# Layer 1 of a two-layer attention and expert network: splitting the expert weights beside the routing and straight into their slots, and a ring of three banks in its attention

## What is computed

```python
qkv = x @ w_qkv.T
o = _natten2d(q / D_HEAD ** 0.5, k, v, KSIZE)          # softmax over 7 x 7 keys
x = x + o @ w_out.T
...
shared_out = (silu(xf @ Wg_s) * (xf @ Wu_s)) @ Wd_s
logits = xf @ W_router + expert_bias
top_vals, top_idx = jax.lax.top_k(logits, 2)
rw = softmax(top_vals)
out_e = (silu(xf @ Wg_r[e]) * (xf @ Wu_r[e])) @ Wd_r[e]   # 384 -> 2 x 768 -> 384
routed_out = sum over the two chosen e of rw * out_e
```

## Time and profile before

| | us |
|---|---|
| median of three runs (1055.34 to 1055.71) | 1055.59 |
| the profiled execution | 1051.15 |
| its span, first to last instruction | 1049.4 |
| TensorE busy (93%) | 973.8 |
| VectorE / GpSimd / ScalarE busy | 544.5 / 519.5 / 322.8 |
| mean granted clock of TensorE | 0.978 |

### The profile page before, as it was taken

One profiled execution on the slowest core, in us unless ns is written; L12 is line 12 of the kernel. 1 busy time (PEld: TensorE's weight loads), 2 busy tenths in 40 slices (PEclk: granted clock), 3 DMA queues, 4 the chain that ended last, 5 costly groups with the idle time before them and its releaser, 6 DMA issues.

```text
span 1049.4 us, 14337 instructions
## 1 busy us (share of the span) xinstructions
PE 973.8 (93%) x4756; PEld 641.0 (61%) x4757; DVE 544.5 (52%) x960; ACT 322.8 (31%) x482; POOL 519.5 (50%) x375
## 2 busy tenths in 40 slices
PE   6999999999998999998598989699899999999998
PEld 3755555555546566665456555368666677677764
DVE  4466888888665355554555675871122222222224
ACT  2524455655721122221325555051111111111100
POOL 5614778898821122220634766646667667700014
PEclk9999999999998999999899999889999999999999
DMA  9679708000056357311435200504777777731015
GB/s 318 161 190 336 168 1 181 21 1 1 1 192 243 130 189 242 144 61 36 128 98 126 62 1 8 218 1 169 259 255 256 255 260 265 255 123 42 16 51 152
DMA packets 52493, 147.43 MB, mean 140 GB/s; under 512 B 7153, under 2 KB 26105, under 8 KB 52184
## 3 DMA queue, kind: packets, MB, share of 16 engines
q1 hardware_dynamic: 37080, 80.00, 25.1%
...
## 4 chain that ended last, share of the span: by engine, by line
PE 66%; POOL 13%; DVE 8%; DMA 7%; issue 4%; ACT 3%; DVEq 0%; SPq 0%; POOLq 0%; ACTq 0%
PE PS L2111 15%; PE PS L2133 8%; POOL raw L1026 6%; PE PS L1838 6%; PE PS L1874 6%; PE PS L1737 5%; PE PS L1894 5%; DMA raw<-in_Wg_r 5%; PE PS L1876 5%; PE PS L2016 3%; PE PS L2159 3%; POOL Wgu L1024 2%; DVE nmax L1426 2%; PE PS L1803 2%; PE PS L1748 2%
## 5 line engine op out<-in xcount | busy, mean ns | idle before, releaser
L1224 ACT ACTIVATE expS<-PS 128x1024 f32<-128x1024 f32 (+3 forms) x156 | 135.3, 877 | 106.4 <-PE PS L1876 104.8
L2133 PE MATMUL PS<-Wd,hidT 128*128 x414 | 142.8, 491 | 1.7 <-DVE hidT L1624 1.0
L953 POOL TENSOR_TENSOR exp_acc<-exp_acc,expS 128x512 f32<-128x512 f32 (+1 forms) x65 | 135.2, 2089 | 16.4 <-ACT expS L1224 14.7
L1874 PE MATMUL PS<-QA,KS 128*128 128x512 f32 (+3 forms) x312 | 116.5, 379 | 4.1 <-ACT QB L1202 3.5
L1426 DVE TENSOR_REDUCE nmax_part<-PS 128x1 f32<-128x512 f32 x160 | 105.5, 682 | 27.6 <-PE PS L1838 27.5
L1838 PE MATMUL PS<-KS,QA 128*128 128x512 f32 (+2 forms) x288 | 108.0, 401 | 9.5 <-DVE nmax L1426 5.1
L1876 PE MATMUL PS<-QB,KS 128*128 128x512 f32 (+3 forms) x312 | 109.9, 358 | 0.0
L2133 PEld LDWEIGHTS PS<-Wd,hidT 128*128 128x128 f32 x414 | 78.8, 192 | 48.9 <-issue 4.1
L2111 PE MATMUL PS<-Wgu,xbT_high 128*128 x207 | 91.1, 440 | 10.6 <-DMA Wgu_low<-raw 7.0
L2111 PE MATMUL PS<-Wgu,xbT 128*128 x276 | 97.4, 490 | 1.8 <-ACT xbT L1321 1.7
L1339 ACT ACTIVATE hidT<-PS 128x384 f32<-128x384 f32 x46 | 22.6, 491 | 236.3 <-PE PS L2119 236.3
...
...
...
## 6 DMA issues: line engine op xcount, KB each, us to landing
...
```

The costliest lines, as they stand in the source:

```text
L953: last = pool.tensor_tensor(acc, older, exp_tile(0, c, u)[:, pair, heads], ALU.add)
L1224: act.activation(exp_tile(layer, c, unit)[:, pair, :].rearrange("p (b n) -> p b n", b=2)[:, :, lo:hi], PS[:, 2 * pair:2 * pair + 2, lo:hi] ...
L1874: pe.matmul(PS[:, 2 * pair + j, lo:hi], keys, QA[layer][c % 2][:, g, queries], start=True, stop=False)
L2133: last = pe.matmul(PS[:, 7, 0:C], hidT[layer][:, par, i, :], Wd[layer][:, bass.ds(s, 1), i, :], start=i == 0, stop=i == m.IC - 1)
```

## The change

In the attention of layer 1 tiles, rows and sums now take turns in banks 4, 5 and 7 by a second list of the same kind. A block's first three tiles move one unit ahead, into unit 4 of the block before (`TILES_TO`; the first block that is made this way keeps `FIRST_TILES`); a unit has one tile behind each head's scores, and the rows stand behind the first pair of heads in unit 3. The reciprocal is cut in four, in units 2, 3 and 4 (two there). Both layers use one function `unit`.

For the expert weights, SyncE loads expert 0's gate weights during the last chunk of the attention (`raw_first_in`). GpSimd splits them once the first half of the tokens is normalised, and the up weights behind the shared expert's subtractions. From expert 1 on the subtraction writes straight into the low slot (`low_of`), no DMA places it, and a raw buffer is loaded again as soon as its part is subtracted; TensorE waits for `low_done`. The slots of high and low parts lie elsewhere for that, with the shared expert's high part now under expert 1's low slot.

```diff
@@ -475,16 +476,13 @@
         LEAD = 2
-        PIECES_TO = [0, 5, 10, 15, 16, 16]
+        FIRST_TILES = [0, 0, 5, 10, 15, 16]
+        TILES_TO = [0, 3, 7, 11, 15, 16]
         ROWS_AT = [6, 3]
         def keys_of(layer, qt):
             return (0, T) if layer == 0 else (max(qt - 1, 0) * P, min(qt + 2, NT) * P)
-
-        def pieces_at(hb, v):
-
-            return range(PIECES_TO[v], PIECES_TO[v + 1])
...
@@ -504,6 +502,11 @@
         def maxima_in(hb, v):
+            if hb >= BLOCKS:
+                ahead = hb + 1 if v < PER_HALF1 - 1 else hb + 2
+                cuts = FIRST_TILES if ahead == BLOCKS + 1 else TILES_TO
+                at = (v + 1) % PER_HALF1
+                return [(ahead, i) for i in range(cuts[at], cuts[at + 1])] if ahead < 2 * BLOCKS else []
...
@@ -513,15 +516,16 @@
             return [(ahead, i) for i in range(pieces(ahead) * at // per_half, pieces(ahead) * (at + 1) // per_half)]
-        ring = [("rows", 0, 0)]
-        for hb in range(BLOCKS):
-            for v in range(PER_HALF):
+        rings = [[("rows", 0, 0)], [("rows", BLOCKS, 0)]]
+        for hb in range(2 * BLOCKS):
+            la, n = hb // BLOCKS, hb % BLOCKS
+            for v in range((PER_HALF, PER_HALF1)[la]):
                 tiles = [("max",) + piece for piece in maxima_in(hb, v)]
-                rows = [("rows", hb + 1, 0)] if v == ROWS_AT[0] and hb + 1 < BLOCKS else []
-                totals = [("sums", hb - 1, 0)] if v == 1 and hb else []
-                ring += tiles[0:1] + tiles[1:2] + rows + tiles[2:4] + totals + tiles[4:]
+                rows = [("rows", hb + 1, 0)] if v == ROWS_AT[la] and n + 1 < BLOCKS else []
+                totals = [("sums", hb - 1, 0)] if v == 1 and n else []
+                rings[la] += tiles[0:2] + rows + tiles[2:4] + totals + tiles[4:]
         RING = [4, 5, 7]
-        ring_at = {item: n for n, item in enumerate(ring)}
+        ring_at = {item: n for ring in rings for n, item in enumerate(ring)}
...
@@ -566,8 +571,8 @@
             return (BLOCKS - 1 + TAIL_CUTS) * (hb // BLOCKS) + hb % BLOCKS
-        CUTS_AT = {3: [0], 4: [1], 5: [2], 6: [3]}
-        CUTS = [len(CUTS_AT), 1]
+        CUTS_AT = [{3: [0], 4: [1], 5: [2], 6: [3]}, {2: [0], 3: [1], 4: [2, 3]}]
+        CUTS = [4, 4]
...
@@ -831,6 +836,8 @@
             check(b_in[0], B_DMAS[1][2])
+            sp.wait_ge(score_psum, 2 * (PV_BEFORE[1] + 2 * U[1]))
+            sp.dma_start(raw_first[:, :, :].bitcast(F32), Wg_r[0].rearrange("(k p) n -> p k n", p=P)).then_inc(raw_first_in, 16)
...
@@ -1010,41 +1017,42 @@
                 def high_of(q, part):
-                    return Wgu[1][:, q % 2, 0, :, part * m.I:(part + 1) * m.I]
+                    return Wgu[1][:, q % 2, :, part * m.I:(part + 1) * m.I]
                 def load_raw(q, part):
                     pool.dma_start(raw_of(q, part)[:, :, :].bitcast(F32),
                                    (Wg_r, Wu_r)[part][q].rearrange("(k p) n -> p k n", p=P)).then_inc(raw_in[part], 16)
+                def low_of(q, part):
+
+                    low = Wgu_low[:, q % 2, 0:KC * 2 * m.I].rearrange("p (k n) -> p k n", k=KC)
+                    return low[:, :, part * m.I:(part + 1) * m.I]
+
                 def split(q, part):
                     own = raw_of(q, part)
-                    pool.wait_ge(raw_in[part], 16 * (q + 1))
+                    if (q, part) == (0, 0):
+                        pool.wait_ge(raw_first_in, 16)
+                    else:
+                        pool.wait_ge(raw_in[part], 16 * (q + part))
                     pool.tensor_copy(high_of(q, part), own[:, :, :].bitcast(F32)).then_inc(high_done, 1)
                     pool.wait_ge(high_done, 2 * q + part + 1)
-                    pool.tensor_tensor(own[:, :, :], own[:, :, :].bitcast(F32), high_of(q, part).bitcast(F32),
-                                       ALU.subtract).then_inc(low_done, 1)
-
-                def place_low(q, part):
-
-                    low = Wgu_low[:, q % 2, 0:KC * 2 * m.I].rearrange("p (k n) -> p k n", k=KC)
-                    pool.wait_ge(low_done, 2 * q + part + 1)
-                    pool.dma_start(low[:, :, part * m.I:(part + 1) * m.I].bitcast(F32), raw_of(q, part)[:, :, :].bitcast(F32)).then_inc(low_placed[part], 16)
-
-                def next_raw(q):
-
-                    for part in range(2):
-                        pool.wait_ge(low_placed[part], 16 * (q + 1))
-                        if q + 1 < E:
-                            load_raw(q + 1, part)
+                    pool.tensor_tensor(low_of(q, part) if q else own[:, :, :], own[:, :, :].bitcast(F32),
+                                       high_of(q, part).bitcast(F32), ALU.subtract).then_inc(low_done, 1)
+
+                def place_first_low(part):
+
+                    pool.wait_ge(low_done, part + 1)
+                    pool.dma_start(low_of(0, part).bitcast(F32), raw_of(0, part)[:, :, :].bitcast(F32)).then_inc(low_placed, 16)
                 def split_and_load(q):
                     for part in range(2):
                         split(q, part)
-                        place_low(q, part)
-                    next_raw(q)
+                        if q + 1 < E:
+                            pool.wait_ge(low_done, 2 * q + part + 1)
+                            load_raw(q + 1, part)
...
@@ -1053,14 +1061,14 @@
                     pool.wait_ge(normalised, normalised_before(2 * BLOCKS - 1) + TAIL_CUTS)
-                    for part in range(2):
-                        load_raw(0, part)
-                    for part in range(2):
-                        split(0, part)
+                    load_raw(0, 1)
+                    pool.wait_ge(xn_ready, 3 * NT + NT // HALF)
+                    split(0, 0)
                     for f in range(m.IC):
...
                                            ALU.subtract).then_inc(gu_lo_ready, 1)
+                    split(0, 1)
...
@@ -1079,8 +1087,10 @@
                     for part in range(2):
-                        place_low(0, part)
-                    next_raw(0)
+                        place_first_low(part)
+                    load_raw(1, 0)
+                    pool.wait_ge(low_placed, 16 * 2)
+                    load_raw(1, 1)
...
@@ -1475,22 +1485,17 @@
                     for v in range(U[layer] // HALF):
+                        for ahead, i in maxima_in(hb, v):
+                            maxima(ahead, [i])
+                            if layer == 0 and i == pieces(ahead) - 1:
+                                merge(ahead)
                         if layer == 0:
-                            for ahead, i in maxima_in(hb, v):
-                                maxima(ahead, [i])
-                                if i == pieces(ahead) - 1:
-                                    merge(ahead)
                             accumulate(hb, v)
-                            if hb > first_block:
-                                for cut in CUTS_AT.get(v, []):
-                                    reciprocals(hb - 1, CUTS[0], [cut])
-                            continue
-                        if hb + 1 < end_block:
-                            maxima(hb + 1, pieces_at(hb + 1, v))
-                            if v == ROWS_AT[1]:
-                                copy_rows(hb + 1)
-                        if v == ROWS_AT[1] and hb > first_block:
-                            reciprocals(hb - 1, 1, range(1))
+                        elif v == ROWS_AT[1] and hb + 1 < end_block:
+                            copy_rows(hb + 1)
+                        if hb > first_block:
+                            for cut in CUTS_AT[layer].get(v, []):
+                                reciprocals(hb - 1, CUTS[layer], [cut])
...
@@ -1846,10 +1848,8 @@
                         pe.wait_ge(max_done, max_before(hb + 1))
-                    bank = 4
-                    if layer == 0:
-                        bank_free(("rows", hb, 0))
-                        bank = ring_bank(("rows", hb, 0))
+                    bank_free(("rows", hb, 0))
+                    bank = ring_bank(("rows", hb, 0))
...
@@ -1963,48 +1966,17 @@
                             tile(2 * pair + j)
-                        if pair == 0 and v == ROWS_AT[0] and hb + 1 < BLOCKS:
+                        if pair == 0 and v == ROWS_AT[layer] and hb + 1 < first_block + BLOCKS:
                             maxima_rows(hb + 1)
                     weighted(c, u)
-                    if v == 1 and hb:
+                    if v == 1 and hb > first_block:
                         totals(hb - 1)
...
                     for u in range(U[layer]):
-                        if layer == 0:
-                            full_unit(c, u)
-                            continue
...
+                        unit(c, u)
...
@@ -2093,15 +2065,15 @@
                         if layer:
-                            for part in range(2):
-                                pe.wait_ge(low_placed[part], (q + 1) * 16)
```

(4 more changed lines are left out.)

75 lines of the change are left out of this document (25 added, 50 removed).

## The result

The changed kernel takes 1024.49 us (median of four runs, 1023.66 to 1025.49), the kernel before beside it 1055.65 (1055.34 to 1057.32): a ratio of 0.9702, 95% interval 0.9685 to 0.9719. Its profiled execution took 1025.49 us for a span of 1023.7.

What follows compares the result with a forecast made beforehand. The prediction took TensorE to bound the kernel nearly everywhere, so its gaps matter. Attention 5.0, expert 0's earlier start 4.6 and experts 10.0 sum to 19.6 us: 1055.59 becomes 1036.0, range 1029 to 1043.

Steps and rivals of the forecast that it cites:

- Part 1: Layer 1's attention: evenly placed VectorE work and earlier rows products remove 5.0 of 8.3 us of TensorE's recorded waits.
- TensorE's own is 17.25 less a fifth of 8.3, some 15.6: Attention block: TensorE's own work is its length less its recorded waits, above VectorE's 13.7 us, so TensorE stays the bound.
- bounds: 0 and 8.3 (no wait is left): Limits of the attention gain in us: VectorE as late at each tile as before, or every recorded wait gone.
- the walk: Stepping through a pair of attention blocks: TensorE 1.1 us ahead of VectorE in each of three blocks, 3.3 us of waits.
- Part 2: Normalisation: the second half's four VectorE instructions run unheld in 1.65 us; the first shared product starts 9.8 us sooner.
- Part 3: Routing: GpSimd's split holds VectorE's ranking, so of the earlier first shared product only 4.6 us reach expert 0.
- the hold misses the routing: Rival for the routing: VectorE gets through more often, expert 0 starts at 734.6, 4.8 us more gain, 1031.2; chance 0.14.
- The queue takes it back: Rival at expert 0: expert 1's load delays the second placement 5.4 us, 14.6 us gain remains, 1041.0; chance 0.10.
- Part 4: Routed experts: low parts go straight to their slots; six blocks take 65.2 us instead of 75.2, 10.0 gained.
- its last wait ends at 819.21: Routed experts before: TensorE waits no more after 819.21 us; blocks then follow every 11.05 us to the end.
- the tightest place: Expert 1: its low parts are done at 759.8 us, just before TensorE wants them at 760.4.
- on the scale of the median 1055.59 − 19.6: Whole kernel: the gain summed against the profiled execution is subtracted unchanged from the timed median, giving 1036.0 us.

## Why the prediction was right in the middle and short at both ends

**Part 1, attention: wrong in size and in reason.** The step that failed is "TensorE's own is 17.25 less a fifth of 8.3, some 15.6", with "bounds: 0 and 8.3 (no wait is left)". Recorded idle time was taken for all that the waits cost. The runs show 9.6 us instead of 5.0: idle time fell by 5.1, and another 4.5 had stood in rows that count as busy. In the block shown above TensorE's own is at most 15.78 less 1.76, 14.0, so by this block the upper bound was nearer 5 x 3.2 = 16 than 8.3.

That the idle part came out at the forecast's 5.0 is luck in part. The sum left out the 1.3 us of waits ahead of the rows, and of the 4.8 that are left (3 to 4 were forecast) 3.0 stand ahead of the rows; at the tiles, where the walk put 3.3, there are 1.8. The walk found a real place (605.04, 1.35 us), but the text looked for the gain in the early tiles, the cut reciprocal and the moved rows. The runs give it to two edits that have no price of their own there: one tile behind each head's scores (5.5) and the third bank (3.9).

The Trainium skill, Perfetto Trace Analysis, section Identifying the Most-Contended Engine, says that the busy share of the matmuls is not a good measure of how close TensorE is to its roofline, since matmuls are pipelined, and takes the busy time of the weight loads among others instead. The trace agrees: when the waits went, the busy time of the same products fell from 100.97 to 96.47 us, and that of their weight loads stayed (66.76 and 66.47).

**Part 2, normalisation: right.** It gave 10.3, where 9.8 were forecast; the four instructions took 1.65, as written, and the granted clock was 1.00 in every stretch of 2 us from 654 to 674, past the router.

**Part 3, the hold in the routing: right.** As forecast, the copy was held to the end of a subtraction and the chain resumed after two more boundaries; the fifth shared product waited 3.45 (3.6 forecast), and 5.2 were given back (5.2). The rival "the hold misses the routing" fell with the three rows of 681.97 to 685.32. The Trainium skill, SBUF — State Buffer, section Who interferes with whom, lets either side wait, by who issued first; here the copy at 685.32, just behind the start of a subtraction at 685.30, was held to its end, 5.14 us in its row. "The queue takes it back" fell too: with the third transfer behind them both placings were there at 728.83, 10.8 after the first one's issue (11.6 forecast).

**Part 4, experts: right, with one row overlooked.** The six blocks took 65.06 for 65.2. The step "its last wait ends at 819.21" was wrong: a wait of 1.12 at 897.95 held the kernel before once more, and that is most of the 1.3 us by which the stage gained beyond the sixth block. The view of who waited for whom, which has four such waits (7.0 us), would have told. Expert 1's low parts were done 17.9 us after expert 0's start (20.4 forecast) and wanted at 20.8, so the tightest place held. One figure of the text doesn't come out: a turn with the slower subtraction, 2 x (2.1 + 7.15 + 0.9), is 20.3 and not 20.7, which changes nothing.

**The scale: the step "on the scale of the median 1055.59 − 19.6" failed.** It took the 4.4 us by which the profiled execution lay below its median for an offset that stays. The four traced executions of before average 2.4 us more than the profiled one in the two stages that end on transfers or behind a long wait (28.87 − 28.05 and 271.67 − 270.09). The change takes those waits out, and with them goes what they add in an ordinary execution: the difference is 26.2 by the four stages on the profiled trace and 28.6 on the four. The 34 timed runs of before, beside the change and beside the experiments, have a median of 1054.8 and the eight of the change one of 1023.9, 30.9 apart. The remaining 2.3 us lie within what the stretch ahead of the change differs by; they were not traced to a place, and their cause stays open.
